# Attention scores of a pre-norm block on one core: each exponential takes three PSUM banks in place of two

## The reference

```
q_weights = exp(q_dists * inv_var)
k_weights = exp(k_dists * inv_var)
logits = einsum('bihs,bjhs,hs->bijh', q_weights, k_weights, amplitudes)
attention = softmax(logits / temp, axis=2)
out = einsum('bijh,bjhd->bihd', attention, v).reshape(Bx, Tx, Dx) @ out_w.T
```

## Time and profile before

| what | value |
|---|---|
| median of 3 runs | 2261.36 us (2261.25 to 2263.63) |
| the profiled execution, its own time | 2263.84 us |
| its span (first to last instruction) | 2261.8 us |
| around the span | 2.0 us |
| granted PE clock, mean | 0.994 of full speed |
| PE busy | 2167.7 us (96%) |
| ACT busy | 2007.1 us (89%) |
| DVE busy | 895.3 us (40%) |

### The profile page before, as it was taken

The page is one execution under the profiler, slowest core; times in us unless marked ns, Lnnn a source line. Parts: engine busy times, 40 slices in busy tenths (PEclk is TensorE's granted clock), DMA queues, the critical chain, the costliest instruction groups (busy, mean ns, idle before and its releaser), DMA issues.

```text
span 2261.8 us, 46282 instructions
## 1 busy us (share of the span) xinstructions
PE 2167.7 (96%) x19886; PEld 897.2 (40%) x19886; DVE 895.3 (40%) x1777; ACT 2007.1 (89%) x2188; POOL 383.2 (17%) x484
## 2 busy tenths in 40 slices
PE   6899999999999999999999999999999999999997
PEld 4333333343444434344443443434433433333344
DVE  5244334425344452532525344352434244214425
ACT  3699999999999998999989899898999999998882
POOL 0242423240120222204022040221300000000000
PEclk9999999999999999999999999999999999999998
DMA  5544325234231433313343222331413130310110
GB/s 152 160 139 100 91 71 129 81 90 118 58 106 41 92 104 81 96 35 103 85 92 104 66 87 62 81 101 34 120 50 81 44 73 27 67 32 17 48 50 19
DMA packets 172799, 180.29 MB, mean 80 GB/s; under 512 B 84992, under 2 KB 110976, under 8 KB 172576
## 3 DMA queue, kind: packets, MB, share of 16 engines
q1 hardware_dynamic: 163312, 162.32, 26.7%
q0 software_dynamic: 7168, 14.69, 2.9%
q10 hardware_dynamic: 2096, 0.14, 0.1%
HBM read 86.45 MB, written 75.89 MB: 72 GB/s over the span
## 4 chain that ended last, share of the span: by engine, by line
PE 77%; ACT 18%; DVE 3%; issue 1%; POOL 1%; DMA 1%; SPq 0%; POOLq 0%; DVEq 0%
PE ps_pv L736 34%; PE ps_scores L719 22%; ACT probs L1044 17%; PE ps_step L764 16%; PE ps_step L781 2%; PE ps_scores L754 1%; PE ps_scores L749 1%; ACT weight L1108 1%; DMA gate_in<-x 1%; DVE o_raw L1359 0%; DVE den_all L1474 0%; POOL packed L1163 0%; PE ps_scores L758 0%; PE ps_scores L759 0%; PE ps_step L743 0%
## 5 line engine op out<-in xcount | busy, mean ns | idle before, releaser
L1044 ACT ACTIVATE probs<-ps_scores 128x1024 f32<-128x1024 f32 x2048 | 1936.5, 1037 | 164.6 <-PE ps_scores L719 158.3
L736 PE MATMUL ps_pv<-probs,vals 128*32 128x512 f32 x8192 | 1068.0, 605 | 12.3 <-DVE o_raw L1359 9.6
L719 PE MATMUL ps_scores<-q_aug,k_aug 49*128 49x512 f32 x4096 | 719.8, 440 | 41.7 <-ACT probs L1044 34.0
L719 PEld LDWEIGHTS ps_scores<-q_aug,k_aug 49*128 49x128 f32 x4096 | 336.0, 185 | 718.9 <-ACT probs L1044 678.6
L736 PEld LDWEIGHTS ps_pv<-probs,vals 128*32 128x32 f32 x8192 | 279.0, 141 | 288.8 <-issue 182.6
L1158 POOL DMA_DIRECT2D packed<-qk x224 | 112.8, 509 | 791.1 <-DVE qk L1292 755.8
L1163 POOL TENSOR_TENSOR packed<-qk 32x512 f32<-32x512 f32 x224 | 236.6, 1056 | 16.9
L1474 DVE RECIPROCAL den_all<-den_all 128x512 f32<-128x512 f32 x63 | 210.9, 3347 | 0.8
L1168 POOL TENSOR_TENSOR k_act<-k_act 128x512 f32<-128x512 f32 x28 | 30.7, 1096 | 978.2 <-DVE k_act L1295 978.2
L1359 DVE COPY o_raw<-ps_pv 128x512 f32<-128x512 f32 x64 | 44.3, 692 | 320.3 <-PE ps_pv L736 320.3
L1292 DVE COPY qk<-ps_step 128x512 f32<-128x512 f32 x56 | 38.7, 691 | 213.1 <-PE ps_step L764 213.1
(11 more groups left out here) (203 smaller groups left out, 1055.2 us busy)
## 6 DMA issues: line engine op xcount, KB each, us to landing
k_aug<-k_parts SPq DMA_DIRECT2D x128, 192.0 KB, 4.8
q_aug<-q_parts SPq DMA_DIRECT2D x128, 192.0 KB
k_parts<-parts SPq DMA_DIRECT2D x32, 512.0 KB, 3.2
q_parts<-parts SPq DMA_DIRECT2D x32, 512.0 KB, 3.4
packed<-qk POOLq DMA_DIRECT2D x224, 64.0 KB, 2.4
x_ffn<-x SPq DMA_DIRECT2D x18, 512.0 KB, 4.2
k_parts<-parts SPq DMA_DIRECT2D x32, 256.0 KB, 4.1
q_parts<-parts SPq DMA_DIRECT2D x32, 256.0 KB, 3.9
```

The lines of the kernel that those rows point to most:

```text
L719: mm = pe.matmul(ps_scores[:, g % RING, e, :], k_aug[rows, s % 2, pair, kt * P:(kt + 1) * P], q_aug[rows, u % 2, pair, :], start=True, sto ...
L736: mm = pe.matmul(ps_pv[32 * c:32 * c + 32, :], vals[:, s % 2, kt, :, c], probs[:, tick % PROB_SLOTS, c, :], start=(kt == 0), stop=(kt == K ...
L1044: act.activation(probs[:, tick % PROB_SLOTS, 2 * pair:2 * pair + 2, :], ps_scores[:, g % RING, :, :], ACT.Exp).then_inc(probs_ready, 1)
```

## The change

The ring is cut by banks and not by pairs. `scores(j)` issues a single matmul into bank `j % 6`. Before the first and the fourth of the six in a gap PE waits for an exponential (the one that last read those three banks), and the third and the sixth signal `scores_ready`. ACT takes three banks, 1536 columns, in one instruction, two to a gap. 4096 banks give 1365 exponentials of three banks and one of a single bank, where there were 2048 of two. A tick of four banks is then no whole number of instructions, so `probs` becomes a ring of 15 single banks in place of 16, and the counts that others wait for are worked out by division (`scored`). The number of matmuls, of columns and of value products is unchanged.

```diff
+SCORE_BANKS = 6
+EXP_BANKS = 3
+PROB_SLOTS = 5 * EXP_BANKS
...
+        def scored(ticks):
+            return -(-HEADS * ticks // EXP_BANKS)
...
-                for e in range(2):
-                    rows = slice(64 * e, 64 * e + ROWS)
-                    mm = pe.matmul(ps_scores[:, g % RING, e, :], k_aug[rows, s % 2, pair, kt * P:(kt + 1) * P],
-                                   q_aug[rows, u % 2, pair, :], start=True, stop=True)
-                mm.then_inc(scores_ready, 1)
+                rows = slice(64 * e, 64 * e + ROWS)
+                return pe.matmul(ps_scores[:, j % SCORE_BANKS, :], k_aug[rows, s % 2, pair, kt * P:(kt + 1) * P],
+                                 q_aug[rows, u % 2, pair, :], start=True, stop=True)
...
-                pe.wait_ge(probs_ready, 2 * tick + 2)
+                pe.wait_ge(probs_ready, (HEADS * tick + HEADS - 1) // EXP_BANKS + 1)
...
-                for g in range(3 * gap, min(3 * gap + 3, 2 * TICKS)):
-                    if g >= RING:
-                        pe.wait_ge(probs_ready, g - RING + 1)
-                    scores(g)
+                for j in range(SCORE_BANKS * gap, min(SCORE_BANKS * (gap + 1), SCORES)):
+                    if j >= SCORE_BANKS and j % EXP_BANKS == 0:
+                        pe.wait_ge(probs_ready, j // EXP_BANKS - 1)
+                    mm = scores(j)
+                    if j % EXP_BANKS == EXP_BANKS - 1 or j == SCORES - 1:
+                        mm.then_inc(scores_ready, 1)
...
-                act.activation(probs[:, tick % PROB_SLOTS, 2 * pair:2 * pair + 2, :], ps_scores[:, g % RING, :, :],
-                               ACT.Exp).then_inc(probs_ready, 1)
+                act.activation(probs[:, at:at + count, :], ps_scores[:, bank:bank + count, :], ACT.Exp).then_inc(probs_ready, 1)
...
-                for g in range(3 * gap, min(3 * gap + 3, 2 * TICKS)):
-                    exponentials(g)
+                for three in range(2 * gap, min(2 * gap + 2, scored(TICKS))):
+                    exponentials(three)
```

More of the change, by code:

```diff
@@ L25 @@
 TICKS = UNITS * KT
-RING = 3
-PROB_SLOTS = 4
+SCORE_BANKS = 6
+EXP_BANKS = 3
+PROB_SLOTS = 5 * EXP_BANKS
+SCORES = HEADS * TICKS
 SAFE_BOUND = 60.0
@@ L361, in preln_block @@
         vals = sb("vals", [P, 2, KT, 2 * S, HEADS])
-        probs = sb("probs", [P, PROB_SLOTS, HEADS, CHUNK])
+        probs = sb("probs", [P, PROB_SLOTS, CHUNK])
         o_raw = sb("o_raw", [P, 2, CHUNK])
@@ L397, in preln_block @@
         max_rows = sb("max_rows", [HEADS, P], F32R)
-        ps_scores = ctx.enter_context(nc.psum_tensor("ps_scores", [P, RING, 2, CHUNK], F32))
+        ps_scores = ctx.enter_context(nc.psum_tensor("ps_scores", [P, SCORE_BANKS, CHUNK], F32))
         ps_pv = ctx.enter_context(nc.psum_tensor("ps_pv", [P, CHUNK], F32))
         ps_step = ctx.enter_context(nc.psum_tensor("ps_step", [P, CHUNK], F32))
-        banks = [ps_scores[:, n // 2, n % 2, :] for n in range(6)] + [ps_pv[:, :], ps_step[:, :]]
+        banks = [ps_scores[:, n, :] for n in range(SCORE_BANKS)] + [ps_pv[:, :], ps_step[:, :]]
         ps_setup = banks[FIRST_NO["dist_k0"] % 8]
@@ L572, in max_pass @@
                     if u >= 2:
-                        sp.wait_ge(scores_ready, 2 * KT * (u - 1))
+                        sp.wait_ge(scores_ready, scored(KT * (u - 1)))
                     if stage == 0:
@@ L655, in _ @@
                     if before in FINAL_UNIT:
-                        sp.wait_ge(scores_ready, 2 * KT * (FINAL_UNIT[before] + 1))
+                        sp.wait_ge(scores_ready, scored(KT * (FINAL_UNIT[before] + 1)))
                         sp.wait_ge(pv_done, FINAL_UNIT[before] + 1)
@@ L707, in _, with scores @@
         def _(pe):
-            def scores(g):
-                u, kt, pair = g // (2 * KT), g % (2 * KT) // 2, g % 2
+            def scores(j):
+                tick, c = divmod(j, HEADS)
+                u, kt = divmod(tick, KT)
+                pair, e = divmod(c, 2)
                 b, s, _ = UNIT[u]
-                if g % (2 * KT) == 0:
+                if kt == 0 and c == 0:
                     pe.wait_ge(q_loaded[u % 2], LOADS_Q * (u // 2 + 1))
@@ L714, in scores @@
                         pe.wait_ge(k_loaded[s % 2], LOADS_K * NC * stage_count(b, s))
-                if u == 0 and pair == 0 and kt % TT == 0:
+                if u == 0 and c == 0 and kt % TT == 0:
                     pe.wait_ge(k_loaded[0], LOADS_K * (kt // TT + 1))
-                for e in range(2):
-                    rows = slice(64 * e, 64 * e + ROWS)
-                    mm = pe.matmul(ps_scores[:, g % RING, e, :], k_aug[rows, s % 2, pair, kt * P:(kt + 1) * P],
-                                   q_aug[rows, u % 2, pair, :], start=True, stop=True)
-                mm.then_inc(scores_ready, 1)
+                rows = slice(64 * e, 64 * e + ROWS)
+                return pe.matmul(ps_scores[:, j % SCORE_BANKS, :], k_aug[rows, s % 2, pair, kt * P:(kt + 1) * P],
+                                 q_aug[rows, u % 2, pair, :], start=True, stop=True)
             def values(tick):
@@ L735, in values @@
                 for c in range(HEADS):
-                    mm = pe.matmul(ps_pv[32 * c:32 * c + 32, :], vals[:, s % 2, kt, :, c], probs[:, tick % PROB_SLOTS, c, :],
+                    mm = pe.matmul(ps_pv[32 * c:32 * c + 32, :], vals[:, s % 2, kt, :, c], probs[:, (HEADS * tick + c) % PROB_SLOTS, :],
                                    start=(kt == 0), stop=(kt == KT - 1))
@@ L1039, in _, with exponentials @@
                 act.dma_start(out=to, in_=of).then_inc(consts_loaded, 16)
-            def exponentials(g):
-                act.wait_ge(scores_ready, g + 1)
-                tick, pair = g // 2, g % 2
-                act.activation(probs[:, tick % PROB_SLOTS, 2 * pair:2 * pair + 2, :], ps_scores[:, g % RING, :, :],
-                               ACT.Exp).then_inc(probs_ready, 1)
+            def exponentials(three):
+                first = EXP_BANKS * three
+                count = min(EXP_BANKS, SCORES - first)
+                at, bank = first % PROB_SLOTS, first % SCORE_BANKS
+                act.wait_ge(scores_ready, three + 1)
+                act.activation(probs[:, at:at + count, :], ps_scores[:, bank:bank + count, :], ACT.Exp).then_inc(probs_ready, 1)
             def copy(name, to, func=ACT.Copy):
@@ L1514, in _ @@
                 rows = x_ffn[:, n % 2, 2 * pair:2 * pair + 2, :]
-                v.tensor_tensor(rows, ps_scores[:, pair, :, 0:D], rows, ALU.add).then_inc(last_evicted, 1)
+                v.tensor_tensor(rows, ps_scores[:, 2 * pair:2 * pair + 2, 0:D], rows, ALU.add).then_inc(last_evicted, 1)
             for part in (0, 1):
```

## The result

The changed kernel takes 2348.95 us (median of 4 runs, 2345.32 to 2350.38) against 2261.31 us before, a ratio of 1.0385 with a 95% interval of 1.0367 to 1.0403. That is 87.6 us slower, and 8 us less than forecast. The profiled execution took 2349.59 us with a span of 2347.6, so 85.8 us of the difference lie inside the span.

The account below looks back on a forecast made before the run. It took a two-gap loop through PE and ACT to bound light gaps and PE's own order full ones. 68 us for light and 37 for full pairs, less 9, gave +96: 2357 us median, range 2308 to 2402.

Parts of the forecast that it names:

- The price of an exponential: On ACT, 1536 columns take 1.34 us in a row, 1.46 alone; a gap needs 0.06 less, 42 us in all.
- (a): ACT starts on the first trio 0.24 us later; PE goes on 3.63 behind block start t, against 3.45: +0.18.
- light pair: Odd gap with little side work, plus the even gap behind it: +0.41 us each, 166 of them, 68 us.
- (b): On PE, half the block waits, not a third: wait to value products 0.66 us in place of 0.43, +0.23.
- (c): PE asks for banks earlier: behind a full gap the trio is 0.11 us late, its block 0.10 longer; every second gap.
- Full pairs: Odd gap with three or four quarters of side work, plus the even gap behind: +0.21 us each, 176, 37 us.
- rival of covered full gaps: Full gaps keep their cover, so the earlier wait costs nothing there: 2320 us; chance 17%.
- full gaps that pay like light ones: If three-bank exponentials end 0.1 us later, full pairs of gaps pay 0.41 too: 2392 us; chance 12%.
- A wash: The lone third matmul costs nothing on ACT's or PE's side: within 0.2% of 2261 us; chance 4%.
- The sum: Whole loop: 68 us from light and 37 from full pairs of gaps, 105, less 5 and 4: +96 us.
- the 9 that I took off: Off the 105 us: 5 for stretches held by DVE, POOL and DMA, 4 for light pairs not waiting before.
- ACT as the bound: Rival: ACT sets the pace of the whole loop, so 42 us go: 2219 us; chance 6%.

Follow-up runs that it names:

- four-two cut: The changed kernel with each gap's six banks cut as four and two in place of two trios, ring of 16 banks: 2291.07 us.
- run with the early wait: The kernel before, with PE's wait for the third pair of scores moved ahead of the second pair, nothing changed on ACT: 2304.06 us.
- e9: The kernel before, with an even gap's first value tick between second and third score pair, only behind odd gaps without side work: 2255.58 us.

## Why the prediction was right

**The price of an exponential** held to the hundredth: 1.45 us for 1536 columns and 2.79 for two in a row, so 1.34 apart (1.46 and 1.34 forecast). ACT's score exponentials came down by 40.0 us (42).

**(a)** Start at t + 0.76 and PE's release at t + 3.61 (0.78 and 3.63). The four-two cut puts (a) at 0.17 a light pair (0.18).

**(b)** 0.66 us from the wait to the value products, in the changed kernel and in the run with the early wait; 0.23 a light pair, as forecast. This was the term with the wide bounds, and the value nearest to the rows of second pairs was right.

**(c)** Full pairs lose 0.19 us (0.21), nearly all in the even gap (27.0 of the 32.0 us in sum), so every second gap pays. In the median the fourth matmul of that even gap starts 0.08 late (0.11) and the stretch behind it to the value products is 0.10 longer (0.10). The rival of covered full gaps is refuted by the run with trios in full gaps alone, 39 us slower, and that of full gaps that pay like light ones by the 0.19. A wash is out by the 0.76 and the 0.66: the lone matmul costs time on both sides.

**The sum** was 96 where the medians differ by 87.6. Full pairs give 32.0 us (37), light ones 52.3 (68 less the 9 that I took off for all). The mis-sized term is the number of light pairs that pay the whole loop. In 28 of the 164, ACT has a tanh or an exponential of the distances to do behind the exponentials of the gap just before. These lose 0.13 in the median and 4.0 us in sum; the other 136 lose 0.39 and 48.4 in sum. In those 28 the first exponential already came late before the change, 0.87 behind the start of the block in the median and 0.78 after it, where the others have 0.54 and 0.77. So (a) costs them nothing and (b) is most of what is left. The prediction's own example, the loop from 956.69 with its 0.27, is one of them and lost 0.06. The 9 that I took off had been put down to DVE and to pairs near the edge, and no run shows that split.

**ACT as the bound** is refuted: 40 us less of ACT, and 87.6 us more of time.

**What I got wrong in the signs to look for.** I expected ACT's share of the chain to rise to a third or more; it fell from 18% to 16%. The share of the score matmuls rose instead, from 22% to 26%: the chain walks back along PE as long as PE's rows touch, and so books the longer blocks on PE. I also expected PE to show idle time before the fourth matmul in full stretches; there the wait of 0.08 us is inside the block of six, 1.16 long.

## What to carry to other kernels

When two engines pass a ring of buffers to each other, write down the loop: from first write to first read, through the reads, from the last release to the first thing that is behind it. Larger pieces save instruction starts on one engine (here 0.06 us a gap) and lengthen the loop at both ends, where it costs the filling of a piece each time (0.24 and 0.23). Before making the pieces larger, see how far the earlier request eats the slack of the stretches that do not wait yet; and if PE must wait, look for work that doesn't need what it waits for, but leave the other engine enough pieces to live on meanwhile.

## What the runs showed of the hardware

- A lone score matmul of 49 rows x 512 columns behind a pair costs what a second pair costs: the value products start 0.66 us behind a wait with three matmuls in the way and with four.
- Exponentials out of PSUM over two, three and four banks lie on one line. 1.03 and 1.45 us alone for 1024 and 1536 columns, 1.34 apart for 1536; one of 1024 and one of 2048 in a row last 2.79 together, in either order, as do two of 1536.
- Behind an idle PE (1.97 us before, 2.48 in e9) the granted clock was 0.50 for the next 2.8 us in both traces. In the pair of gaps after that it was 0.99 before and 0.59 in e9, and the pair took 5.79 and 8.20 us.
